# State-space stage: five of eight B products on GpSimd after the scans, three on VectorE from PSUM, and no pair additions

## The chip, the cores and the metric

The kernel is one launch on one core of a Trainium2 chip. The metric is the device time of a launch in microseconds; the kernel before took 2772.1 us in the median of 3 runs (2766.68 to 2773.61). The engines are called as the profile calls them: PE (TensorE, matrix products), PEld (its weight loads), DVE (VectorE), ACT (ScalarE), POOL (GpSimd), SP (SyncE, here the queue of transfers).

## The reference, cut to what matters

The whole is a decoder of two layers on x of 16 sequences x 112 steps x 256 features: a state-space layer, cross attention, a mixture of experts, an encoder, a second cross attention with a long convolution, and a coupled network. The change touches the first stage only:

```python
dt = softplus(x[:, :, 0:1] * W_dt + b_dt)
BC = einsum('bld,ed->ble', x, W_xp) + b_xp
Bm, Cm = BC[..., :16], BC[..., 16:]
# for every step t of a sequence
state = exp(A * dt_t) * state + dt_t * x_t * B_t     # 256 features x 16 states
y = einsum('bdn,bn->bd', state, C_t)
out = y @ W_out + b_out                              # then residual and layer norm
```

## The kernel before, in words

The stage is cut into eight units. A unit is one half c of the 256 features (128 partitions) and one quarter q of the 16 sequences (4 sequences x 112 steps = 448 columns): unit 0 is (c=0, q=0), unit 1 (c=1, q=0), unit 2 (c=0, q=1) and so on. "Even units" have c=0, "odd units" c=1. The 16 states of a unit lie side by side in `st_h` (two buffers, by the parity of the unit), and are handled as eight pairs of 896 columns.

For each unit:

- PE broadcasts the rows of B, one pair of states at a time, over 128 partitions into PSUM (L478, a matmul of a one-hot column with `bc_parts`). There is one such ring of two slots in PSUM, for B and for C (`RING`); a broadcast waits until the one two places before it has been used. ACT copies all eight B pairs to SBUF (`b_s`, L578), once per quarter, in the odd unit before. Only for unit 0 does DVE read the B pairs straight from the ring (L701).
- POOL multiplies the eight B pairs with u = dt * x (L774, u is kept in `XD`) and writes them into `st_h`. It does so for unit i+1 at the start of unit i.
- ACT computes the decays exp(A dt) into `dA` (L588, 16 instructions), which are needed by the next unit and wait for this unit's scans.
- DVE runs the recurrence as two scans of eight states (L682, 3584 columns), then multiplies eight pairs with C out of the ring (L718).
- POOL adds the two states of a pair for six of the eight pairs (L781, `ADDED` = 6).
- PE sums the states of the unit by matmuls with the identity into one bank of PSUM (L492): one matmul for each added pair and two for each of the other two, 10 in all. It does this at the start of the next unit, after that unit's first two B broadcasts, if it has any.

After the sum PE does the unit's window of other work (`shared_uses`): in even units the products z and bc for the next quarter (L412, L418), in units 4 and 6 also transposes (L462), and in all units the keys and values of two sequences for the next stage (L430, L440). In odd units the remaining B broadcasts stand between them. The last work of the unit is the C broadcasts; in odd units from 3 on, the projection W_out (L453) stands after the second of them (`late_uses`), and DVE adds the residual and takes the statistics (L732, L265, L268) before its C products.

In even units ACT turns z into a part of dt (L534, L535, L538) and copies bc (L549, L550); the logarithms of the softplus (L544) stand behind the window. DVE splits bc into bfloat16 parts between its two scans (L661 to L663, `split`) and computes dt and u after the C products (L670, L672, `step_sizes`, four instructions for the two units of the next quarter). The first two work on bc's 64 rows, the others on 128 x 448.

The order on each engine is written out by hand; the engines meet at semaphores. `ssm_claim` deals three banks of PSUM in turn to the products of the window, so one of them waits until the third before it has been copied.

Of the kernel before, what the change touches and what calls it, by code (L numbers as in the profile page):

```python
# [20 lines left out]
P = 128  # L21
# [13 lines left out]
def build(nc, dr, out):  # L35

    ctx = ExitStack()
    with ctx:
# [185 lines left out]
        pair_added = sem("pair_added")  # L224
# [66 lines left out]
        HALF, ADDED = 8, 6  # L291
# [38 lines left out]
        def copied_b(i):  # L330

            c, q = UNITS[i]
            if i == 0:
                return [(0, pair) for pair in range(8)]
            return [(q + 1, pair) for pair in range(8)] if c == KC - 1 and q + 1 < NQ else []
# [29 lines left out]
        for i in range(len(UNITS)):  # L365
            RING += [("b", x) for x in copied_b(i)] + [("c", (i, pair)) for pair in range(8)]
        RING_AT = {u: n for n, u in enumerate(RING)}
        SSM_USES = [("z", 0), ("z", 1), ("bc", 0)]
# [5 lines left out]
        def ring_wait(eng, kind, at):  # L374

            i, pair = at
            if kind == "direct":
                eng.wait_ge(bcast_used, pair + 1)
            elif kind == "c":
                eng.wait_ge(bcast_used, 8 + 8 * i + pair + 1)  # L380
            else:
                eng.wait_ge(b_copied, 8 * i + pair + 1)
# [25 lines left out]
        def ssm_pe(pe):  # L408
# [60 lines left out]
            def broadcast(kind, at):  # L469

                n = RING_AT[(kind, at)]
                if n >= 2:
                    ring_wait(pe, *RING[n - 2])
                i, pair = at
                q, first = (UNITS[i][1], 16) if kind == "c" else (i, 0)
                for m in range(2):
                    s = first + 2 * pair + m
                    last = pe.matmul(ps[2 * (n % 2) + m][:, 0:QT], ident16[0:96, s:s + 1].to_broadcast([96, P]),  # L478
                                     bc_parts[0:96, q % 2, :], start=True, stop=True)
                last.then_inc(bcast_ready, 1)  # L480

            def sum_states(i):

                for pair in range(8):
                    if pair < ADDED:
                        pe.wait_ge(pair_added, i * ADDED + pair + 1)
                    else:
                        pe.wait_ge(bcast_used, 8 + 8 * i + pair + 1)
                    if pair == 0 and i >= 1:
                        pe.wait_ge(y_copied, i)  # L490
                    for m in range(1 if pair < ADDED else 2):
                        last = pe.matmul(ps[4][:, 0:QT], ident[:, :], st_h[:, i % 2, 2 * pair + m, :],  # L492
                                         start=(pair == 0 and m == 0), stop=(pair == 7 and m == 1))
                    last.then_inc(y_ready, 1)
# [9 lines left out]
            for i, (c, q) in enumerate(UNITS):  # L504
# [15 lines left out]
                for pair in range(2, 8):  # L520
                    broadcast("c", (i, pair))
            for k in range(KC):
                turn(KC * (NQ - 2) + k)
# [4 lines left out]
        def ssm_act(act):  # L528
# [43 lines left out]
            def copy_b(at):  # L572
                q, pair = at
                n = RING_AT[("b", at)]
                act.wait_ge(bcast_ready, n + 1)
                if q >= 1:
                    act.wait_ge(b_mult, 16 * (q - 1) + pair + 1)
                act.copy(b_s[:, 2 * pair:2 * pair + 2, :], PS[:, 2 * (n % 2):2 * (n % 2) + 2, 0:QT])\  # L578
                    .then_inc(b_copied, 1)
# [18 lines left out]
            copies = {"z": magnitude, "bc": copy_both, "k": copy_keys, "v": copy_values, "xt": copy_turned}  # L598
# [12 lines left out]
            for i, (c, q) in enumerate(UNITS):  # L611
# [9 lines left out]
                if c == 0 and q + 1 < NQ:  # L621
                    logarithm(2 * q + 2)
                    logarithm(2 * q + 3)
# [31 lines left out]
        def ssm_dve(dve, link):  # L655
# [18 lines left out]
            def scan(i, half):  # L674
# [4 lines left out]
                else:  # L679
                    dve.wait_ge(b_mult, 8 * (i - 1) + 4 * (half + 1))  # L680
                h = st_h[:, i % 2, n, :].rearrange("p n k -> p (n k)")
                dve.tensor_tensor_scan(h, dA[:, n, :, :].rearrange("p n b t -> p (n b t)"), h, 0.0,  # L682
                                       ALU.mult, ALU.add).then_inc(scan_done, 1)

# [11 lines left out]
            u2 = u_f[:, 0:1, 0:QT].to_broadcast([P, 2, QT])  # L696
            dve.wait_ge(u_done, 1)
            for pair in range(8):
                n = RING_AT[("direct", (0, pair))]
                dve.wait_ge(bcast_ready, n + 1)  # L700
                dve.tensor_tensor(st_h[:, 0, 2 * pair:2 * pair + 2, :], PS[:, 2 * (n % 2):2 * (n % 2) + 2, 0:QT],  # L701
                                  u2, ALU.mult).then_inc(bcast_used, 1)
            step_sizes(1)
            for i, (c, q) in enumerate(UNITS):
# [3 lines left out]
                scan(i, 1)  # L708
                if late_uses(i):
# [37 lines left out]
        def ssm_pool(pool, link):  # L747
# [17 lines left out]
            for i in range(len(UNITS)):  # L765
                if i + 1 < len(UNITS):
# [3 lines left out]
                    for pair in range(8):  # L770
                        pool.wait_ge(b_copied, 8 * q + pair + 1)
# [23 lines left out]
        def xat_load(sp):  # L795
            sp.wait_ge(b_mult, 8 * (len(UNITS) - 1))
# [1856 lines left out]
```

## Time and profile before

| | |
|---|---|
| median of 3 runs | 2772.1 us (2766.68 to 2773.61) |
| profiled execution, its own time | 2774.99 us |
| its span | 2773.1 us |
| mean granted clock of PE | 0.823 |
| PE busy | 2245.8 us (81%) |
| DVE busy | 1609.1 us (58%) |
| POOL busy | 894.5 us (32%) |
| ACT busy | 736.0 us (27%) |
| state-space scans on DVE (L682) | 181.8 us in 16 instructions |
| B products on POOL (L774) | 166.4 us in 56 instructions |

Busy time is that in which an engine has an instruction under way, also while that instruction is held up at a port. The shares are means over stages that differ: the stage of the change ends some 360 us after the start of the span, and only its own waits say what bounds it. An instruction's time in brackets is the idle time of its engine before it, with what ended it.

### The profile page before, as it was taken

What the parts mean: (1) busy time and instruction counts of PE and PEld (TensorE: products, weight loads), DVE (VectorE), ACT (ScalarE), POOL (GpSimd) and SP (SyncE); (2) the same over time, 40 slices, a digit from 0 to 9 for tenths busy, and PEclk for the clock granted to TensorE, in tenths of its full rate; (3) what the DMA queues carried; (4) which work ended last, traced back from release to release, by engine and by line L of the source; (5) the groups of instructions that cost most, each with busy time, mean ns of one, the idle gap of its engine ahead of it and who ended that gap; (6) DMA issues with size and microseconds to landing.
All of it is one profiled execution on the core that took longest, in us unless ns stands there. A gap on an engine that the chain in (4) does not pass through costs nothing.

```text
span 2773.1 us, 36682 instructions
## 1 busy us (share of the span) xinstructions
PE 2245.8 (81%) x14852; PEld 1568.3 (57%) x14852; DVE 1609.1 (58%) x3034; ACT 736.0 (27%) x1387; POOL 894.5 (32%) x715
## 2 busy tenths in 40 slices
PE   7787778888787999799999999988657775866776
PEld 2343345566565666578888887776445453434432
DVE  7888834444442333355565655666399997555345
ACT  6545322222221121222222222222222221211122
POOL 7787349816110000534444343442200002111000
PEclk7888866656556999799999999999766767788987
DMA  4212213111111000100100100100150101400000
GB/s 133 80 50 79 80 43 106 34 51 34 40 32 46 1 1 1 73 1 1 60 2 1 60 1 1 45 1 1 54 103 26 34 26 28 94 0 0 1 0 27
DMA packets 63473, 100.52 MB, mean 36 GB/s; under 512 B 32301, under 2 KB 56870, under 8 KB 62150
## 3 DMA queue, kind: packets, MB, share of 16 engines
q1 hardware_dynamic: 63306, 98.18, 12.2%
q8 instruction: 119, 1.95, 0.3%
q14 instruction: 48, 0.39, 0.0%
HBM read 77.67 MB, written 20.50 MB: 35 GB/s over the span
## 4 chain that ended last, share of the span: by engine, by line
PE 62%; DVE 25%; DMA 4%; ACT 3%; issue 3%; POOL 3%; SPq 0%; POOLq 0%; DVEq 0%; ACTq 0%
PE PS L1421 7%; PE PS L1437 7%; PE PS L1177 4%; DVE st_h L682 4%; DVE top L2175 3%; PE PS L883 3%; PE PS L1156 3%; DVE w_s L2184 3%; PE PS L1338 3%; DMA enc_w<-v_all_scratch 3%; PE PS L896 2%; DVE XD L1038 2%; PE PS L2061 2%; DVE ln_st L265 2%; PE PS L933 2%
## 5 line engine op out<-in xcount | busy, mean ns | idle before, releaser
L284 POOL TENSOR_SCALAR ln_ve<-ln_mv 128x2 f32<-128x2 f32 (+1 forms) x91 | 20.2, 222 | 1523.4 <-DVE ln_mv L268 1523.4
L883 PE MATMUL PS<-enc_w,q_s 17*112 17x375 f32 x512 | 188.1, 795 | 78.0 <-DVE XD L1038 59.8
L1613 DVE TENSOR_TENSOR p_x<-PS,cols 128x1024 f32<-128x1024 f32 x112 | 129.3, 1218 | 147.7 <-PE PS L1383 147.6
L1038 DVE TENSOR_REDUCE XD<-PS 112x2 f32<-112x750 f32 x128 | 120.3, 940 | 161.0 <-PE PS L883 161.0
L1675 POOL TENSOR_TENSOR q_x<-q_f,cols 128x2048 f32<-128x2048 f32 x56 | 208.6, 3744 | 9.7 <-ACT q_f L1533 9.7
L682 DVE TENSOR_TENSOR_SCAN st_h<-dA,st_h 128x3584 f32<-128x3584 f32 x16 | 181.8, 11388 | 0.0
L896 PE MATMUL PS<-q_s,enc_w 17*125 17x112 f32 x1536 | 180.1, 388 | 1.1 <-ACT e_t L1006 1.1
L1006 ACT ACTIVATE e_t<-PS 125x672 f32<-125x672 f32 x128 | 93.6, 731 | 312.8 <-PE PS L896 312.8
L774 POOL TENSOR_TENSOR st_h<-b_s,XD 128x896 f32<-128x896 f32 x56 | 166.4, 3009 | 8.0 <-PE PS L492 6.8
L896 PEld LDWEIGHTS PS<-q_s,enc_w 17*125 17x125 f32 x1536 | 151.2, 279 | 2.1 <-issue 2.0
L1241 DVE SCALAR_TENSOR_TENSOR XA<-PS,gate_w,XA 112x256 f32<-112x256 f32 x128 | 61.9, 484 | 135.4 <-PE PS L1177 135.4
L1945 PE MATMUL PS<-dg,e_p 112*125 112x112 f32 x384 | 82.4, 409 | 71.3 <-ACT dg L2129 71.3
L883 PEld LDWEIGHTS PS<-enc_w,q_s 17*112 17x112 f32 x512 | 59.4, 250 | 131.9 <-DVE XD L1038 85.4
L478 PE MATMUL PS<-bc_parts,ident 96*128 96x448 bf16 x208 | 78.3, 478 | 62.2 <-DVE st_h L718 54.3
L1503 ACT ACTIVATE wb<-PS,cols 128x256 f32<-128x256 f32 x224 | 91.0, 473 | 141.1 <-PE PS L1421 141.1
L1945 PEld LDWEIGHTS PS<-dg,e_p 112*125 112x125 f32 x384 | 79.1, 320 | 82.9 <-issue 82.9
L1177 PE MATMUL PS<-wc,h_t 128*112 128x256 f32 x512 | 119.2, 388 | 2.4 <-DVE XA L1244 2.4
L1421 PE MATMUL PS<-wc 128*128 128x256 f32 x448 | 105.6, 396 | 10.4 <-ACT wc L1548 10.4
L1177 PEld LDWEIGHTS PS<-wc,h_t 128*112 128x112 f32 x512 | 92.4, 181 | 33.0 <-issue 14.3
L1421 PE MATMUL PS<-wc,enc_w 128*128 128x256 f32 x448 | 100.4, 382 | 9.5 <-ACT wc L1548 9.5
L1156 PE MATMUL PS<-XF,wc 128*128 128x448 f32 x256 | 103.6, 549 | 0.7 <-DVE gate_wt L1230 0.7
L1421 PEld LDWEIGHTS PS<-wc 128*128 128x128 f32 x448 | 87.6, 198 | 26.4 <-ACT wc L1548 14.0
(351 smaller groups left out, 4959.3 us busy)
## 6 DMA issues: line engine op xcount, KB each, us to landing
v_all_scratch<-v_st SPq DMA_DIRECT2D x16, 750.0 KB
enc_w<-v_all_scratch SPq DMA_DIRECT2D x16, 750.0 KB
t_ring<-k_scratch SPq DMA_DIRECT2D x8, 784.0 KB, 11.5
enc_w<-in_enc_w SPq DMA_DIRECT2D x2, 3072.0 KB, 10.4
wc<-in_enc_w SPq DMA_DIRECT2D x2, 3072.0 KB, 10.9
k_all_scratch<-k_st SPq DMA_DIRECT2D x16, 375.0 KB
enc_w<-k_all_scratch SPq DMA_DIRECT2D x64, 93.8 KB
ctx_k<-in_ctx SPq DMA_DIRECT2D x16, 281.2 KB
```

What stands on the lines that cost most here:

```text
L682: dve.tensor_tensor_scan(h, dA[:, n, :, :].rearrange("p n b t -> p (n b t)"), h, 0.0, ALU.mult, ALU.add).then_inc(scan_done, 1)
L774: pool.tensor_tensor(st_h[:, (i + 1) % 2, 2 * pair:2 * pair + 2, :], b_s[:, 2 * pair:2 * pair + 2, :], u2, ALU.mult).then_inc(b_mult, 1)
L883: ins = pe.matmul(ps[a][0:T, 0:S2], q_s[h, m, b * T:(b + 1) * T], k_s[h, b % 2, m, :], start=True, stop=True)
L896: ins = pe.matmul(ps[2 + a][0:JR, j * T:(j + 1) * T], k_s[h, b % 2, m, j * JR:(j + 1) * JR], q_s[h, m, b * T:(b + 1) * T], start=True, sto ...
L1038: dve.tensor_reduce(nm_w[0:T, g % 2, 64 * half + 16:64 * half + 49:32], PS[0:T, 0:2, 0:S2], AX.X, ALU.max, negate=True).then_inc(max_done, 1)
L1156: last = pe.matmul(ps[pair + m][:, 0:QT], w1_e[:, e, k, m * P:(m + 1) * P], XF[:, k, q * QT:(q + 1) * QT], start=(k == 0), stop=(k == KC - 1))
L1177: last = pe.matmul(bank, h_t[:, i % 2, k, b * T:(b + 1) * T], w2_e[:, e, k, :], start=(k == 0), stop=(k == KC - 1))
L1421: last = pe.matmul(ps[bank][:, (m % 2) * RT:(m % 2 + 1) * RT], w[:, k, m * P:(m + 1) * P], x1f[:, i % 2, k, :], start=(k == 0), stop=(k == ...
L1437: last = pe.matmul(ps[3][:, g * D:(g + 1) * D], h_ff[:, m, g * P:(g + 1) * P], w[:, m, :], start=(m == 0), stop=(m == 7))
L1613: last = dve.tensor_tensor(p_x[:, m, :, :, :], ps[1][:, m * P:(m + 1) * P].rearrange("p (h i) -> p h i", i=16).unsqueeze(2) .to_broadcast( ...
L1675: last = pool.tensor_tensor(q_x[:, c, :, :].rearrange("p t (h i) -> p t h i", i=16), q_f[:, k % 2, c, :].rearrange("p (t i) -> p t i", i=1 ...
L1945: last = pe.matmul(bank[0:JR, j * T:(j + 1) * T], e_p[:, XH * (b % 2) + h, j * JR:(j + 1) * JR], dg[:, b % 2, h, :], start=(h == 0), stop= ...
```

## The change

What it does:

- POOL takes five B pairs of each unit (`COPIED` = 5) and starts them only after both scans of the unit before are done (a wait on `scan_done`). DVE takes the other three from the ring in PSUM, right after its C products of the unit before (`multiply_b`). ACT copies five B pairs a quarter in place of eight.
- The pair additions on POOL and their semaphore are gone. PE sums 16 states by 16 matmuls.
- In even units the two logarithms are computed right after the second `magnitude`, ahead of the copy of bc, and `step_sizes` stands on DVE after the second scan, ahead of the C products.

```diff
@@ -288,7 +287,7 @@
-        HALF, ADDED = 8, 6
+        HALF, COPIED = 8, 5
...
         for i in range(len(UNITS)):
             RING += [("b", x) for x in copied_b(i)] + [("c", (i, pair)) for pair in range(8)]
+            if i + 1 < len(UNITS):
+                RING += [("direct", (i + 1, pair)) for pair in range(COPIED, 8)]
...
             def sum_states(i):
 
                 for pair in range(8):
-                    if pair < ADDED:
-                        pe.wait_ge(pair_added, i * ADDED + pair + 1)
-                    else:
-                        pe.wait_ge(bcast_used, 8 + 8 * i + pair + 1)
+                    pe.wait_ge(bcast_used, DVE_AT[("c", (i, pair))] + 1)
                     if pair == 0 and i >= 1:
                         pe.wait_ge(y_copied, i)
-                    for m in range(1 if pair < ADDED else 2):
+                    for m in range(2):
...
                 for pair in range(2, 8):
                     broadcast("c", (i, pair))
+                if i + 1 < len(UNITS):
+                    for pair in range(COPIED, 8):
+                        broadcast("direct", (i + 1, pair))
...
+            def magnitude_and_log(i):
+                magnitude(i)
+                if i % KC == KC - 1:
+                    logarithm(i - 1)
+                    logarithm(i)
+
-            copies = {"z": magnitude, "bc": copy_both, "k": copy_keys, "v": copy_values, "xt": copy_turned}
+            copies = {"z": magnitude_and_log, "bc": copy_both, "k": copy_keys, "v": copy_values, "xt": copy_turned}
...
-                if c == 0 and q + 1 < NQ:
-                    logarithm(2 * q + 2)
-                    logarithm(2 * q + 3)
                 if i + 1 < len(UNITS):
                     decay(i + 1, 0)
                     decay(i + 1, 1)
...
+            def multiply_b(i, pair):
+                c, q = UNITS[i]
+                at = RING_AT[("direct", (i, pair))]
+                if i >= 2:
+                    dve.wait_ge(y_ready, 8 * (i - 2) + pair + 1)
+                dve.wait_ge(bcast_ready, at + 1)
+                dve.tensor_tensor(st_h[:, i % 2, 2 * pair:2 * pair + 2, :], PS[:, 2 * (at % 2):2 * (at % 2) + 2, 0:QT],
+                                  u_f[:, c:c + 1, q * QT:(q + 1) * QT].to_broadcast([P, 2, QT]), ALU.mult)\
+                    .then_inc(bcast_used, 1)
...
                 scan(i, 1)
+                if c == 0 and q + 1 < NQ:
+                    step_sizes(2 * q + 2)
+                    step_sizes(2 * q + 3)
...
                     dve.tensor_tensor(h, PS[:, 2 * (n % 2):2 * (n % 2) + 2, 0:QT], h, ALU.mult)\
                         .then_inc(bcast_used, 1)
-                if c == 0 and q + 1 < NQ:
-                    step_sizes(2 * q + 2)
-                    step_sizes(2 * q + 3)
+                if i + 1 < len(UNITS):
+                    if i == 0:
+                        dve.wait_ge(u_done, 2)
+                    for pair in range(COPIED, 8):
+                        multiply_b(i + 1, pair)
...
                     pool.wait_ge(u_done, i + 2)
-                    for pair in range(8):
-                        pool.wait_ge(b_copied, 8 * q + pair + 1)
+                    pool.wait_ge(scan_done, 2 * (i + 1))
+                    for pair in range(COPIED):
+                        pool.wait_ge(b_copied, COPIED * q + pair + 1)
...
-                for pair in range(ADDED):
-                    h0, h1 = st_h[:, i % 2, 2 * pair, :], st_h[:, i % 2, 2 * pair + 1, :]
-                    pool.wait_ge(bcast_used, 8 + 8 * i + pair + 1)
-                    pool.tensor_tensor(h0, h0, h1, ALU.add).then_inc(pair_added, 1)
```

The order of DVE's instructions in unit 4 (even) up to the first scans of unit 5, before (L682 is the scan):

```order
L682 SCALAR_TENSOR_TENSOR st_h<-dA,st_h 128x3584
L661 TENSOR_TENSOR bc_f<-bc_f,bc_parts 64x448
L662 CAST bc_parts<-bc_f 64x448
L663 TENSOR_TENSOR bc_parts<-bc_f,bc_parts 32x448
L682 SCALAR_TENSOR_TENSOR st_h<-dA,st_h 128x3584
L718 TENSOR_TENSOR st_h<-PS,st_h 128x896 x8
L670 TENSOR_TENSOR dt_f<-dt_f,XD 128x448
L672 TENSOR_TENSOR XD<-dt_f,XF 128x448
L670 TENSOR_TENSOR dt_f<-dt_f,XD 128x448
L672 TENSOR_TENSOR XD<-dt_f,XF 128x448
L682 SCALAR_TENSOR_TENSOR st_h<-dA,st_h 128x3584 x2
```

and the same place of the changed kernel (L687 is the scan, L664 to L666 the split, L673 and L675 the step sizes, L732 the C products, L696 the B products from PSUM):

```order
L687 SCALAR_TENSOR_TENSOR st_h<-dA,st_h 128x3584
L664 TENSOR_TENSOR bc_f<-bc_f,bc_parts 64x448
L665 CAST bc_parts<-bc_f 64x448
L666 TENSOR_TENSOR bc_parts<-bc_f,bc_parts 32x448
L687 SCALAR_TENSOR_TENSOR st_h<-dA,st_h 128x3584
L673 TENSOR_TENSOR dt_f<-dt_f,XD 128x448
L675 TENSOR_TENSOR XD<-dt_f,XF 128x448
L673 TENSOR_TENSOR dt_f<-dt_f,XD 128x448
L675 TENSOR_TENSOR XD<-dt_f,XF 128x448
L732 TENSOR_TENSOR st_h<-PS,st_h 128x896 x8
L696 TENSOR_TENSOR st_h<-PS,XD 128x896 x3
L687 SCALAR_TENSOR_TENSOR st_h<-dA,st_h 128x3584 x2
```

The step sizes moved ahead of the C products, three B products came in behind those, and the split stands where it stood, between the scans.

ACT in the window of unit 4, before (L534 to L538 the second magnitude, L549 and L550 the copies of bc, L570 those of the transposes):

```order
L534 ACTIVATE XD<-PS,cols 128x448
L535 ACTIVATE dt_f<-PS,cols 128x448
L538 ACTIVATE XD<-XD 128x448
L549 ACTIVATE bc_parts<-PS,cols 96x448
L550 ACTIVATE bc_f<-PS,cols 64x448
L570 COPY XF<-PS 128x448 x2
```

and after (L544 are the logarithms):

```order
L534 ACTIVATE XD<-PS,cols 128x448
L535 ACTIVATE dt_f<-PS,cols 128x448
L538 ACTIVATE XD<-XD 128x448
L544 ACT_TABLE_LOAD
L544 ACTIVATE XD<-XD 128x448 x2
L549 ACTIVATE bc_parts<-PS,cols 96x448
L550 ACTIVATE bc_f<-PS,cols 64x448
L570 COPY XF<-PS 128x448 x2
```

A table load and the two logarithms now stand ahead of the copies of bc.

PE from the end of unit 4 to the first C broadcasts of unit 5, before (L478 are broadcasts, two to a pair; L492 the sum):

```order
L478 MATMUL PS<-bc_parts,ident 128x448 x20
L492 MATMUL PS<-st_h,ident 128x448 x10
L478 MATMUL PS<-bc_parts,ident 128x448 x2
L430 MATMUL PS<-ctx_t,wb 128x375 x2
L478 MATMUL PS<-bc_parts,ident 128x448 x2
L430 MATMUL PS<-ctx_t,wb 128x375 x2
L478 MATMUL PS<-bc_parts,ident 128x448 x2
L440 MATMUL PS<-wb,ctx_t 125x256 x4
L478 MATMUL PS<-bc_parts,ident 128x448 x2
L440 MATMUL PS<-wb,ctx_t 125x256 x2
```

and after (the sum is L489):

```order
L478 MATMUL PS<-bc_parts,ident 128x448 x26
L489 MATMUL PS<-st_h,ident 128x448 x16
L478 MATMUL PS<-bc_parts,ident 128x448 x2
L430 MATMUL PS<-ctx_t,wb 128x375 x2
L478 MATMUL PS<-bc_parts,ident 128x448 x2
L430 MATMUL PS<-ctx_t,wb 128x375 x2
L478 MATMUL PS<-bc_parts,ident 128x448 x2
L440 MATMUL PS<-wb,ctx_t 125x256 x6
```

The run of broadcasts ahead of the sum is longer by three pairs, the sum by six matmuls, and the window has three B broadcasts (pairs) in place of six.

## Rows read from the trace of the kernel before

**Rows 1.** Timeline of DVE, units 4 to 6: start, length, what, idle before.

```profile
188.37 26.11 DVE L682 TENSOR_TENSOR_SCAN st_h<-dA,st_h 128x3584 f32<-128x3584 f32 x1
214.40 0.59 DVE L661 TENSOR_TENSOR bc_f<-bc_f,bc_parts 64x448 f32<-64x448 f32 x1
...
215.98 7.61 DVE L682 TENSOR_TENSOR_SCAN st_h<-dA,st_h 128x3584 f32<-128x3584 f32 x1
223.52 8.47 DVE L718 TENSOR_TENSOR st_h<-PS,st_h 128x896 f32<-128x896 f32 x8
231.90 0.62 DVE L670 TENSOR_TENSOR dt_f<-dt_f,XD 128x448 f32<-128x448 f32 x1
...
234.29 16.98 DVE L682 TENSOR_TENSOR_SCAN st_h<-dA,st_h 128x3584 f32<-128x3584 f32 x2
258.48 0.76 DVE L732 TENSOR_TENSOR XA<-PS,XA 112x256 f32<-112x256 f32 x2 [7.21 <-PE PS L453]
...
262.66 8.47 DVE L718 TENSOR_TENSOR st_h<-PS,st_h 128x896 f32<-128x896 f32 x8
271.05 34.25 DVE L682 TENSOR_TENSOR_SCAN st_h<-dA,st_h 128x3584 f32<-128x3584 f32 x2
```

**Rows 2.** Timeline of POOL in unit 4.

```profile
190.65 16.34 POOL L774 TENSOR_TENSOR st_h<-b_s,XD 128x896 f32<-128x896 f32 x8
```

**Rows 3.** Timeline of DVE: the first scans of units 1, 2, 3 and 7.

```profile
67.69 16.95 DVE L682 TENSOR_TENSOR_SCAN st_h<-dA,st_h 128x3584 f32<-128x3584 f32 x2
...
106.22 24.98 DVE L682 TENSOR_TENSOR_SCAN st_h<-dA,st_h 128x3584 f32<-128x3584 f32 x1
...
151.01 16.98 DVE L682 TENSOR_TENSOR_SCAN st_h<-dA,st_h 128x3584 f32<-128x3584 f32 x2
...
313.60 15.13 DVE L682 TENSOR_TENSOR_SCAN st_h<-dA,st_h 128x3584 f32<-128x3584 f32 x2
```

**Rows 4.** Timeline of PE, units 4 and 5: sums, windows, C broadcasts.

```profile
187.12 9.94 PE L492 MATMUL PS<-st_h,ident 128*128 128x448 f32 x20
196.98 1.77 PE L412 MATMUL PS<-XF,rows 1*128 1x448 f32 x4
...
202.34 3.35 PE L430 MATMUL PS<-ctx_t,wb 128*128 128x375 f32 x8 [0.91 <-ACT bc_f L550]
...
214.22 0.92 PE L478 MATMUL PS<-bc_parts,ident 96*128 96x448 bf16 x4
...
232.76 9.30 PE L492 MATMUL PS<-st_h,ident 128*128 128x448 f32 x20
241.90 0.54 PE L478 MATMUL PS<-bc_parts,ident 96*128 96x448 bf16 x2
...
255.72 0.92 PE L478 MATMUL PS<-bc_parts,ident 96*128 96x448 bf16 x4
```

**Rows 5.** Windows of L492 alone: length, PE busy, PEld busy, granted clock, DMA.

```profile
237.00:241.90 4.90, 4.90 (x14) 2.28 (x12) 1.00 0.00 0
...
187.20:190.00 2.80, 2.80 (x4) 1.27 (x4) 0.50 0.00 0
```

**Rows 6.** Timeline of ACT in unit 4: magnitudes, copies of bc, logarithms.

```profile
198.04 0.63 ACT L534 ACTIVATE XD<-PS,cols 128x448 f32<-128x448 f32 x1 [0.41 <-PE PS L412]
...
201.05 0.63 ACT L549 ACTIVATE bc_parts<-PS,cols 96x448 bf16<-96x448 f32 x1
201.57 0.63 ACT L550 ACTIVATE bc_f<-PS,cols 64x448 f32<-64x448 f32 x1
...
214.81 1.28 ACT L544 ACT_TABLE_LOAD   x1
216.11 1.04 ACT L544 ACTIVATE XD<-XD 128x448 f32<-128x448 f32 x2
```

**Rows 7.** Timeline of DVE in unit 0: the split beside POOL's B products.

```profile
39.61 1.98 DVE L661 TENSOR_TENSOR bc_f<-bc_f,bc_parts 64x448 f32<-64x448 f32 x1 [2.42 <-ACT bc_f L550]
...
43.82 2.39 DVE L663 TENSOR_TENSOR bc_parts<-bc_f,bc_parts 32x448 bf16<-32x448 f32 x1
46.14 7.60 DVE L682 TENSOR_TENSOR_SCAN st_h<-dA,st_h 128x3584 f32<-128x3584 f32 x1
```

More of the change, by code:

```diff
@@ L223, in build @@
         ones_set = sem("ones_set")
-        pair_added = sem("pair_added")
         dA_ready, scan_done = sem("dA_ready"), sem("scan_done")
@@ L333, in copied_b @@
             if i == 0:
-                return [(0, pair) for pair in range(8)]
-            return [(q + 1, pair) for pair in range(8)] if c == KC - 1 and q + 1 < NQ else []
+                return [(0, pair) for pair in range(COPIED)]
+            return [(q + 1, pair) for pair in range(COPIED)] if c == KC - 1 and q + 1 < NQ else []
         def shared_uses(i):
@@ L366, in build @@
             RING += [("b", x) for x in copied_b(i)] + [("c", (i, pair)) for pair in range(8)]
+            if i + 1 < len(UNITS):
+                RING += [("direct", (i + 1, pair)) for pair in range(COPIED, 8)]
         RING_AT = {u: n for n, u in enumerate(RING)}
+        DVE_AT = {u: n for n, u in enumerate(u for u in RING if u[0] != "b")}
         SSM_USES = [("z", 0), ("z", 1), ("bc", 0)]
@@ L376, in ring_wait @@
             i, pair = at
[L377 to L380, printed above, removed]
+            if kind == "b":
+                eng.wait_ge(b_copied, COPIED * i + pair + 1)
             else:
-                eng.wait_ge(b_copied, 8 * i + pair + 1)
+                eng.wait_ge(bcast_used, DVE_AT[(kind, at)] + 1)
         def ssm_bank(kind, i):
@@ L474, in broadcast @@
                 i, pair = at
-                q, first = (UNITS[i][1], 16) if kind == "c" else (i, 0)
+                q, first = (i if kind == "b" else UNITS[i][1]), (16 if kind == "c" else 0)
                 for m in range(2):
@@ L576, in copy_b @@
                 if q >= 1:
-                    act.wait_ge(b_mult, 16 * (q - 1) + pair + 1)
+                    act.wait_ge(b_mult, COPIED * 2 * (q - 1) + pair + 1)
                 act.copy(b_s[:, 2 * pair:2 * pair + 2, :], PS[:, 2 * (n % 2):2 * (n % 2) + 2, 0:QT])\
@@ L679, in scan @@
                 else:
-                    dve.wait_ge(b_mult, 8 * (i - 1) + 4 * (half + 1))
+                    dve.wait_ge(b_mult, COPIED * (i - 1) + min(4 * (half + 1), COPIED))
+                    if half == 1:
+                        dve.wait_ge(bcast_used, DVE_AT[("direct", (i, 7))] + 1)
                 h = st_h[:, i % 2, n, :].rearrange("p n k -> p (n k)")
@@ L695, in ssm_dve @@
             step_sizes(0)
-            u2 = u_f[:, 0:1, 0:QT].to_broadcast([P, 2, QT])
             dve.wait_ge(u_done, 1)
             for pair in range(8):
[L699 to L702, printed above, removed]
+                multiply_b(0, pair)
             step_sizes(1)
@@ L795, in xat_load @@
         def xat_load(sp):
-            sp.wait_ge(b_mult, 8 * (len(UNITS) - 1))
+            sp.wait_ge(b_mult, COPIED * (len(UNITS) - 1))
             for i in range(2):
```

## The prediction

> **What bounds the kernel now.** I read the timeline of DVE first, then those of PE, ACT and POOL at the same places. Times inside a unit are counted from the start of its first scan, called t = 0; the span from one unit's first scan to the next is its period.
>
> The reader is to see in [rows 1] that even units and odd units have different limits. Unit 4 (even) is bound by DVE: its first scan takes 26.11 us where the second takes 7.61, because POOL's eight B products, back to back for 16.34 us [rows 2], stand in between; everything on DVE follows without a gap, and the period is 234.29 - 188.37 = 45.9 us. In unit 5 (odd) the two scans take 16.98 us (POOL is the one that is held up), and then DVE idles 7.21 us for the projection [rows 1]. PE bounds it: the sum starts at 232.76, a window without holes follows, and C products start at 262.66 [rows 4, 1]. Its period is 36.8 us. The other starts of scans [rows 3, 1] give periods of 38.5 (unit 1), 44.8 (unit 2), 37.4 (unit 3) and 42.6 (unit 6). So a gain at the port counts in units 2, 4 and 6 alone, and work added to PE counts in all odd ones.
>
> **The sizes.** One state matmul shows as two records. At the full clock 4.90 us hold about 13 whole records [rows 5], 0.38 each, 0.76 us a matmul; at half clock four records take 2.80 us or more, twice that. The sums before, 10 matmuls in 9.94 and 9.30 us [rows 4], start at half clock and end at full clock. The six matmuls that are added come behind, at full clock: 6 x 0.76 = 4.6 us a unit. A DVE product from PSUM takes 8.38 / 8 = 1.05 us (223.52 to 231.90), also while POOL is at work; three more are 3.15 us. A B broadcast in the window shows 0.54 us [rows 4], part of it over its neighbour's time; I take 0.4, so three fewer give back 1.2 us in units 1, 3 and 5.
>
> **Odd units.** The direct products are at the end of DVE's order, and PE's sum stands behind their broadcasts, so the sum of the unit just ended cannot start before they are nearly done. In unit 5 before, the sum began 0.86 us after the C products' end (231.90), while DVE spent 2.39 us on the step sizes before its scan: PE had that head start. With the step sizes moved, the scan follows the last product at once, and PE lacks it. Change of period: 2.4 (head start gone) + 4.6 (matmuls) - 1.2 (broadcasts) + 3.15 (products after the C products) = +8.9 us, for units 3 and 5. From 36.8 to 45.7: DVE's scans, free of POOL, end at 15.2 and buy nothing. POOL's five products run from 15.2 to 25.6 and are hidden. Unit 1 has no projection or statistics. Its sum starts at 0.9 and takes 9.1 + 4.6, the window is 255.72 - 241.90 - 1.2 = 12.6, the first C broadcast 0.5, and 11 products 11.55: 39.3 us, +0.8 on 38.5, since PE there also waited for POOL's additions before.
>
> **Even units.** The scans are free, but the split between them waits for bc, and bc comes behind the sum on PE and, now, behind the logarithms on ACT. Before, in unit 4, the sum started at -1.25 and z at 8.6; bc's last copy ended at 202.20, t = 13.8 [rows 4, 6], hidden by the long first scan. After: 13.8 + 4.6 (matmuls) + 2.3 (table load and two logarithms, 214.81 to 217.15 [rows 6], which now stand before the copies) = 20.7. DVE ends its first scan at 7.6 and then waits 13 us. This is the main step of this prediction: the stall at the port is replaced by a stall at bc. Then the split takes 1.6 (214.40 to 215.98; POOL now waits for the second scan, so it is not disturbed), and the second scan 7.5: 29.9. At that moment POOL starts five products, and the four step sizes (0.62 us each alone [rows 1]) run beside them. In unit 0 before, three small DVE instructions beside such products took from 39.61 to 46.14, 2.18 us each [rows 7]. I take the first as free, 0.65, and three at 2.2: 7.25. The C products start at 37.1. PE is ready: its keys wait for bc's copy as the 0.91 us before them show [rows 4], so the first C broadcast ends at 20.7 + (214.22 + 0.54 - 202.20 = 12.6) = 33.3. Eleven products, 11.55, end the unit at 48.7. The period of unit 4 grows by 2.8, that of unit 2, the same sum against 44.8, by 3.9.
>
> The step sizes have two ends: alone they take 2.5 us, and the C products then start at PE's 33.3 in unit 4 (-3.8 us) and at 32.4 in unit 2 (-4.7); if DVE is kept out until all five are through (as the scan of 26.11 was for 16.34), they take 0.65 + 5 x 2.04 + 3 x 0.62 = 12.7, +5.5 a place. I stay with [rows 7], the same two kinds of instruction side by side.
>
> The Trainium skill has this rule (SBUF — State Buffer, "SBUF: two separate sides"): a DVE instruction with two inputs in SBUF and a GpSimd instruction take turns at a shared port, whoever starts first holds it for the whole instruction. This case's rows agree for the scan; for the short ones, a full turn of POOL before each of four would give 4 x (2.04 + 0.62) = 10.7 us in place of 7.25, some 3.4 more in each of three units. The measured pitch of 2.18 decides.
>
> **The ends of the stage.** Unit 0: before, DVE waited 2.42 us for bc and split from 39.61 [rows 7]. The 2.3 us of logarithms are partly hidden there (ACT itself waited for PE; between 0 and 2.3, I take 1.1): 40.7, + 1.6 + 7.5 = 49.8, + 7.25 = 57.1, + 11.55 = 68.6 against 67.69: +0.9. Unit 6 has no z, no bc and no split. PE: -1.25 + 9.9 + 4.6 + the window of unit 4 without z, bc and the wait (214.22 - 196.98, less 3.3 for z's 1.77 and as much for bc, overlapping, less 0.9: 13.0) + 0.4 = 26.7, + 11.55 = 38.3 against 42.6: -4.3. Here alone the freed port pays. Unit 7 has no direct products: +4.6; the sum of unit 7 after it: +4.6.
>
> **The sum.** 0.9 + 0.8 + 3.9 + 8.9 + 2.8 + 8.9 - 4.3 + 4.6 + 4.6 = +31.1 us. On the profiled execution's 2774.99 (span 2773.1 and 1.9 around it) that is 2806; it lay 2.9 above the median, so for the median 2772.1 + 31.1 = 2803. Nothing behind the stage changes; its start is simply late. The decays are hidden: in even units ACT starts them when the window ends, near 33, plus a table load of 1.3 and 9 us of work, 44 < 48.7.
>
> **The rivals.**
> - *Step sizes undisturbed, clock sooner back* (same mechanism, low end). POOL starts late enough or gives way: -4.7, -3.8, and -4.7 in unit 0. That is +17.9. If the sums also ran at full clock from the start, which no sum before did, the most is the excess over 7.6 us, about 2 us in each of eight: +2.
> - *Step sizes locked out, or the clock held low by PE's longer idle* (high end). Three times +5.5 from above: +47.6. For the clock: in unit 4 PE now idles for bc some 3 us more in its window, and if half of a window of 12 us went at half clock, it would add 6, of which 4 are hidden by the step sizes.
> - *Faster: the port decides.* If the excess of the first scans came free, 17.4 us in unit 2 (24.98 - 7.61), 18.5 in unit 4 and 19.1 in unit 6 (34.25 less two free scans), that is 55 us; against it stand the 28.7 of the other terms and three products more in each of the three, 9.5. That would give -17, 2755. It decides only if bc is there before 7.6. Against it: the sum of 16 alone takes until 13.2 even by these rows, and PE's order puts z and bc behind it. It would need PE to sum in a third of the time. The mild form, bc ready at 18 and all else at its best, is the +2 above.
> - *Nothing to see.* Between +2 and +8, where every loss meets its low end.
>
> **How the numbers follow.** Forecast with its own range of 2795 to 2812: 0.62. Low rival (2780 to 2795): 0.18. High rival (above 2812): 0.11. Nothing to see, within 0.3% or 8.3 us, about what a measurement can tell: 0.06. Faster: 0.03. The range for 8 in 10 is 2787 to 2815. Slower 0.91, same 0.06, faster 0.03.
>
> **What would show it.** In the profile of the changed kernel: all 16 scans near 7.6 us; DVE idle before L664 for some 13 us in units 2 and 4, put down to ACT's bc_f; L489 as 32 records in 13 to 15 us; the step sizes at about 2.2 us each but the first; odd periods near 46, even 49, unit 6 near 38. Wrong would be: a split without a wait, step sizes of 0.6 us, or the sum of 16 at under 12 us.

## The result, and the profile after

The changed kernel takes 2809.86 us in the median of 4 runs (2805.92 to 2815.83), the kernel before beside it 2770.59. The ratio is 1.0123, with a 95% interval of 1.0097 to 1.0149, which is 34 us slower (27 to 41); the two medians lie 39 us apart. Forecast were 31 us and a median of 2803, with a range of 2795 to 2812: the measured one lies in the range, near its upper end. The profiled execution has a span of 2808.8 us (before 2773.1, a difference of 35.7).

The stage's end is the end of its last statistics (L268 before, L267 after, in DVE's timeline): 363.13 us before and 398.33 after, +35.2. What follows takes 2410.0 and 2410.5 us. So all but 0.5 us of the difference between the two profiled executions is in the state-space stage. Its periods in us, from the starts of first scans:

| unit | before | forecast | after |
|---|---|---|---|
| 0 | 38.1 | +0.9: 39.0 | 39.6 |
| 1 | 38.5 | 39.3 | 39.9 |
| 2 | 44.8 | 48.7 | 49.1 |
| 3 | 37.4 | +8.9: 46.3 | 46.3 |
| 4 | 45.9 | 48.7 | 50.8 |
| 5 | 36.8 | 45.7 | 45.5 |
| 6 | 42.6 | 38.3 | 37.1 |
| 7 to the stage's end | 49.5 | +9.2: 58.7 | 60.9 |

DVE's timeline of units 4 and 5 after (start, length, what, idle before), which answers to [rows 1]:

```profile
204.01 7.61 DVE L687 TENSOR_TENSOR_SCAN st_h<-dA,st_h 128x3584 f32<-128x3584 f32 x1
224.49 0.62 DVE L664 TENSOR_TENSOR bc_f<-bc_f,bc_parts 64x448 f32<-64x448 f32 x1 [12.87 <-ACT bc_f L550]
...
226.10 7.61 DVE L687 TENSOR_TENSOR_SCAN st_h<-dA,st_h 128x3584 f32<-128x3584 f32 x1
233.64 0.59 DVE L673 TENSOR_TENSOR dt_f<-dt_f,XD 128x448 f32<-128x448 f32 x1
234.26 2.39 DVE L675 TENSOR_TENSOR XD<-dt_f,XF 128x448 f32<-128x448 f32 x1
236.57 2.49 DVE L673 TENSOR_TENSOR dt_f<-dt_f,XD 128x448 f32<-128x448 f32 x1
239.10 2.39 DVE L675 TENSOR_TENSOR XD<-dt_f,XF 128x448 f32<-128x448 f32 x1
243.31 8.20 DVE L732 TENSOR_TENSOR st_h<-PS,st_h 128x896 f32<-128x896 f32 x8 [1.82 <-PE PS L478]
251.60 3.28 DVE L696 TENSOR_TENSOR st_h<-PS,XD 128x896 f32<-128x896 f32 x3
254.79 15.13 DVE L687 TENSOR_TENSOR_SCAN st_h<-dA,st_h 128x3584 f32<-128x3584 f32 x2
284.40 0.76 DVE L748 TENSOR_TENSOR XA<-PS,XA 112x256 f32<-112x256 f32 x2 [14.48 <-PE PS L453]
...
288.58 8.47 DVE L732 TENSOR_TENSOR st_h<-PS,st_h 128x896 f32<-128x896 f32 x8
297.15 3.28 DVE L696 TENSOR_TENSOR st_h<-PS,XD 128x896 f32<-128x896 f32 x3
300.34 15.13 DVE L687 TENSOR_TENSOR_SCAN st_h<-dA,st_h 128x3584 f32<-128x3584 f32 x2
```

The reader is to see the trade: the first scan fell from 26.11 us to 7.61, and 12.87 us of idle time stand behind it, ended by ACT's copy of bc. The step sizes take 2.4 us each but the first. In unit 5 the wait for the projection grew from 7.21 to 14.48 us.

PE's timeline of the same stretch, which answers to [rows 4]:

```profile
202.69 14.26 PE L489 MATMUL PS<-st_h,ident 128*128 128x448 f32 x32
216.88 1.77 PE L412 MATMUL PS<-XF,rows 1*128 1x448 f32 x4
...
224.60 6.23 PE L430 MATMUL PS<-ctx_t,wb 128*128 128x375 f32 x8 [3.28 <-ACT bc_f L550]
230.76 5.48 PE L440 MATMUL PS<-wb,ctx_t 128*125 128x256 f32 x12
...
242.66 0.92 PE L478 MATMUL PS<-bc_parts,ident 96*128 96x448 bf16 x4
...
255.65 13.38 PE L489 MATMUL PS<-st_h,ident 128*128 128x448 f32 x32
268.87 0.54 PE L478 MATMUL PS<-bc_parts,ident 96*128 96x448 bf16 x2
```

The sums take 14.26 and 13.38 us for 16 matmuls, where 10 took 9.94 and 9.30: 4.3 and 4.1 more. Behind the wait for bc PE's keys (L430) take 6.23 us where they took 3.35. A window on them has the reason (length; busy time of PE, PEld, DVE, ACT and POOL; granted clock; DMA share and GB/s):

```profile
224.60:230.80 6.20, 6.20 (x9) 2.01 (x9) 6.13 (x4) 1.27 (x3) 0.00 (x0) 0.50 0.00 0
```

The granted clock is 0.50, which is 1.2 GHz, after 3.28 us without a matmul. Ahead of that wait, from 209 to 221 us, it was 1.00.

ACT at the same place, which answers to [rows 6], has the logarithms ahead of bc:

```profile
221.08 1.28 ACT L544 ACT_TABLE_LOAD   x1
222.38 1.04 ACT L544 ACTIVATE XD<-XD 128x448 f32<-128x448 f32 x2
223.33 0.61 ACT L549 ACTIVATE bc_parts<-PS,cols 96x448 bf16<-96x448 f32 x1
223.84 0.61 ACT L550 ACTIVATE bc_f<-PS,cols 64x448 f32<-64x448 f32 x1
```

And POOL's products in units 4 and 5, which answer to [rows 2]: 11.62 us beside the step sizes, 10.23 alone.

```profile
233.84 11.62 POOL L791 TENSOR_TENSOR st_h<-b_s,XD 128x896 f32<-128x896 f32 x5 [39.48 <-DVE st_h L687]
...
270.05 10.23 POOL L791 TENSOR_TENSOR st_h<-b_s,XD 128x896 f32<-128x896 f32 x5 [24.59 <-DVE st_h L687]
```

### The profile page after: what moved, and what is told of

Same layout as the page of the kernel before. It is cut to its first block, busy times and chain, and to the rows that moved or that the text cites. A ratio compares the mean times of both kernels' runs of the same rounds, so it can differ in the third digit from the quotient of the medians.

```text
span 2808.8 us, 36848 instructions
## 1 busy us (share of the span) xinstructions
PE 2308.5 (82%) x14966; PEld 1594.4 (57%) x14966; DVE 1580.4 (56%) x3055; ACT 724.7 (26%) x1375; POOL 743.0 (26%) x646
## 3 DMA queue, kind: packets, MB, share of 16 engines
q8 instruction: 119, 1.95, 0.3%
## 4 chain that ended last, share of the span: by engine, by line
PE 65%; DVE 22%; ACT 4%; DMA 3%; issue 3%; POOL 2%; SPq 0%; POOLq 0%; DVEq 0%; ACTq 0%
PE PS L1434 7%; PE PS L1450 7%; PE PS L1190 4%; PE PS L489 4%; PE PS L896 3%; DVE top L2188 3%; PE PS L1169 3%; DVE w_s L2197 3%; PE PS L1351 3%; PE PS L909 2%; PE PS L2074 2%; DVE XD L1051 2%; DMA enc_w<-v_all_scratch 2%; PE PS L946 2%; DVE ln_st L264 2%
## 5 line engine op out<-in xcount | busy, mean ns | idle before, releaser
L896 PEld LDWEIGHTS PS<-enc_w,q_s 17*112 17x112 f32 x512 | 60.5, 255 | 130.4 <-DVE XD L1051 85.9
L478 PE MATMUL PS<-bc_parts,ident 96*128 96x448 bf16 x226 | 89.7, 500 | 47.7 <-DVE st_h L732 37.5
L791 POOL TENSOR_TENSOR st_h<-b_s,XD 128x896 f32<-128x896 f32 x35 | 75.9, 2201 | 200.3 <-DVE st_h L687 177.4
L687 DVE TENSOR_TENSOR_SCAN st_h<-dA,st_h 128x3584 f32<-128x3584 f32 x16 | 121.3, 7608 | 0.0
L489 PE MATMUL PS<-st_h,ident 128*128 128x448 f32 x256 | 112.2, 603 | 0.0
```

The lines of the kernel that those rows point to most:

```text
L896: ins = pe.matmul(ps[a][0:T, 0:S2], q_s[h, m, b * T:(b + 1) * T], k_s[h, b % 2, m, :], start=True, stop=True)
```

## The experiments

The span of one profiled execution also moves with what lies behind the stage: 2403 to 2417 us in the fourteen profiled kernels, which differ in the first stage alone. The stage's end is the sharper reading, and each part gives both; ratios are to the kernel before, with 95% intervals. The end comes from one trace of each kernel, so its own spread was not measured. Two things bound it: the first scan starts between 28.56 and 31.18 us, and units that an edit leaves alone repeat closely (units 5, 6 and 7 take 45.6, 37.1 and 60.9 us in the first experiment and 45.5, 37.1 and 60.9 in the changed kernel). Of the versions of the changed kernel, the first three have ratios whose intervals overlap with its own, 1.0097 to 1.0149; what these experiments show, they show in the units.

**The split behind both scans.**

```diff
                 scan(i, 0)
-                if c == 0 and q + 1 < NQ:
-                    split(q + 1)
                 scan(i, 1)
                 if c == 0 and q + 1 < NQ:
+                    split(q + 1)
                     step_sizes(2 * q + 2)
```

> The changed kernel, with the split moved behind both scans (ahead of the step sizes). Theory (in even units DVE stalls for bc between its scans, while the second scan could have run): the second scan runs at once, both end at 15.2 us; the split starts when bc comes, at 20.4; the C products of unit 2 start when PE is ready, near 31 instead of 37.4 (-6 us), unit 0 gains 3.5, unit 4 nothing, since PE's own window ends there at 39.3. Span 2799 (-9). Rival (the wait for bc costs nothing, PE bounds all even units): -0 to -2 us. Rival (the order of the two does not matter, bc is late for what follows in any case): unit 2 unchanged too.

Span 2803.1, stage end 389.69 (-8.6 on the changed kernel), ratio 1.0094 (1.0068 to 1.0121). Unit 2 fell from 49.1 to 40.8 us and unit 4 stayed (50.8 and 51.1). The theory has the direction of both, and 6 us for the 8.3 of unit 2: there the split now took 6.5 us beside POOL, and the step sizes behind it ran alone in 2.5. Unit 0 did not gain its 3.5: there the split and the step sizes both ran beside POOL. The stall at bc between the scans costs in unit 2; in unit 4 PE's slowed window covers it, and DVE waits 10.68 us for the first C broadcast.

**z and bc ahead of the sum.**

```diff
+                order = window_order(i)
+                while i >= 1 and order and order[0][0] in ("z", "bc"):
+                    kind, at = order.pop(0)
+                    shared[kind](at)
                 if i >= 1:
                     sum_states(i - 1)
-                for kind, at in window_order(i):
+                for kind, at in order:
```

(and the same with `copies` and `copy_y` on ACT)

> The changed kernel, with z and bc (PE) and their magnitudes, logarithms and copies (ACT) ahead of the sum of states and the copy of y in units 2, 4 and 6. Theory (bc comes late because it stands behind the sum of 16): bc is there at about 7 us, DVE does not wait between its scans, PE does not idle before the keys and keeps its full clock, and the C products start when PE is ready, near 30. Periods of units 2 and 4 fall from 49.1 and 50.8 to about 41.5: span 2790 (-17 to -19). Rival (the sum's length itself, not its place, is what counts on PE): only the part of DVE's wait that PE's window does not cover, -8.

Span 2798.3, stage end 385.09 (-13.2), ratio 1.0076 (1.0048 to 1.0104). The span is 8 us above the 2790 expected, though units 2 and 4 take 41.8 and 42.9 us, near the 41.5 expected, and DVE no longer idles between its scans. The keys of unit 4 are at full speed again:

```profile
215.94 3.29 PE L430 MATMUL PS<-ctx_t,wb 128*128 128x375 f32 x8
```

The other units gave some of it back (unit 5 takes 46.3 for 45.5, unit 6 37.5 for 37.1), which I did not follow further.

**No wait for the scans on POOL.**

```diff
                     pool.wait_ge(u_done, i + 2)
-                    pool.wait_ge(scan_done, 2 * (i + 1))
```

> The changed kernel without POOL's wait on scan_done: its five products may run into the scans as before the change. Theory (the freed port buys nothing where DVE waits for bc or for PE anyway, and the wait makes the step sizes collide with POOL): scans become longer again by up to 10.4 us in some units, the step sizes fall from 2.4 to 0.6 us each, unit 2 gains about 5 us, the others about 0: span 2803 (-5). Rival (undisturbed scans are worth their time): even periods grow by 5 to 10 us each, span 2825 or more.

Span 2803.6, stage end 390.22 (-8.1), ratio 1.01 (1.0076 to 1.0123). The first scans of units 2 and 4 stay at 7.6 us without the wait (two scans take 16.96 for 15.13 in units 1, 3, 5 and 6). That is more than the theory had said: not even the length of these first scans needed it. Unit 2 gained 5.9 us, with step sizes of 0.6 us each. Within the changed kernel the wait is a loss, by the stage's end; the ratio is too near that of the changed kernel to say it.

**The pair additions back on POOL.**

```diff
-        HALF, COPIED = 8, 5
+        HALF, COPIED, ADDED = 8, 5, 6
...
-                    for m in range(2):
+                    for m in range(1 if pair < ADDED else 2):
...
+                for pair in range(ADDED):
+                    h0, h1 = st_h[:, i % 2, 2 * pair, :], st_h[:, i % 2, 2 * pair + 1, :]
+                    pool.wait_ge(bcast_used, DVE_AT[("c", (i, pair))] + 1)
+                    pool.tensor_tensor(h0, h0, h1, ALU.add).then_inc(pair_added, 1)
```

> The changed kernel with the pair additions back on POOL for six pairs, and 10 matmuls in PE's sum. Theory (six matmuls of 0.76 us stand in the chain of every unit, in odd ones directly, in even ones through bc; POOL can add beside DVE's products from PSUM): every period falls by about 4.6 us, the end too: 8 x 4.6, span 2772 (-37), as before the change. Rival (POOL's additions come late behind its five products and run into the next scans or hold PE's sum up, as in units 0 and 1 of the kernel before): the gain is under 20 us.

Span 2769.2, stage end 359.21 (-39.1), ratio 0.9985 (0.9967 to 1.0002). Units 1 to 6 fell by 4.7, 5.7, 4.7, 5.7, 4.6 and 4.0 us, and unit 7 with the end by 11.4. Unit 0 did not gain (39.8 for 39.6), and its first scan started 1.3 us later. The six extra matmuls of each sum are worth as much as the whole loss, in this kernel. What is left of the change then is hard to tell from the kernel before (the stage ends 3.9 us sooner, the ratio's interval holds 1): units 3 and 5 take 41.6 and 40.9 us for 37.4 and 36.8, units 2 and 6 43.4 and 33.1 for 44.8 and 42.6.

**The kernel before with one part alone: PE sums all 16 states.**

```diff
-        HALF, ADDED = 8, 6
+        HALF, ADDED = 8, 0
...
-                for pair in range(ADDED):
+                for pair in range(0):
```

> The kernel before, with one part of the change alone: PE sums all 16 states and POOL adds no pairs. Theory (the six matmuls stand in the chain of PE-bound units; even units have no use for the time): units 3, 5 and 7 and the end each grow by 4.6 us; even units change only as POOL's products meet the scans otherwise, -2 to -3 each: span 2785 (+12). Rival (the additions on POOL were as costly as the matmuls, by the port): no change or a gain, 2760 to 2773.

The theory missed: 2785 was expected, the span is 2763.4, the stage ends at 356.50 (-6.6 on the kernel before), ratio 0.9989 (0.9973 to 1.0005). The odd units do lose as expected: unit 3 takes 41.0 us for 37.4, unit 5 41.2 for 36.8, unit 7 with the end 60.5 for 49.5. But units 2, 4 and 6 take 40.9, 40.7 and 33.6 us for 44.8, 45.9 and 42.6, and units 0 and 1 gain 3.4 each. The medians do not tell this version from the kernel before. DVE's and POOL's timelines of its unit 2:

```profile
98.78 7.62 DVE L682 TENSOR_TENSOR_SCAN st_h<-dA,st_h 128x3584 f32<-128x3584 f32 x1
116.14 0.76 DVE L661 TENSOR_TENSOR bc_f<-bc_f,bc_parts 64x448 f32<-64x448 f32 x1 [9.74 <-ACT bc_f L550]
```
```profile
100.61 30.31 POOL L774 TENSOR_TENSOR st_h<-b_s,XD 128x896 f32<-128x896 f32 x8 [5.83 <-PE PS L492]
```

The eight products still have no wait for the scans, and they start 1.83 us after the scan, where they started 1.13 us after it in unit 2 of the kernel before (107.35 and 106.22); yet the first scan takes 7.62 us. So it was not the place of the products alone that kept it from the port in the kernel before: POOL was already at work when the scan came, with the additions of the odd unit, and went on into the products without a gap. POOL's timeline of the kernel before, just ahead of the row of [rows 2], shows it (DVE's scan came at 188.37):

```profile
184.11 6.58 POOL L781 TENSOR_TENSOR st_h<-st_h 128x448 f32<-128x448 f32 x6
```

**The logarithms and step sizes back in their old places.**

```diff
             def magnitude_and_log(i):
                 magnitude(i)
-                if i % KC == KC - 1:
-                    logarithm(i - 1)
-                    logarithm(i)
...
+                if c == 0 and q + 1 < NQ:
+                    logarithm(2 * q + 2)
+                    logarithm(2 * q + 3)
                 if i + 1 < len(UNITS):
                     decay(i + 1, 0)
```

(and on DVE `step_sizes` stands behind the three B products again)

> The changed kernel with the logarithms again behind the window on ACT and the step sizes again behind DVE's products. Theory (the logarithms delay bc by 2.3 us in front of a DVE that waits for it, the step sizes stand beside POOL's products at 2.4 us each, and moved ahead they take PE's head start of 2.4 us from every odd unit): unit 0 -3.3, unit 2 -5, unit 4 -6.7, units 1, 3, 5 -2.4 each: span 2787 (-22). Rival (the place of the step sizes is indifferent, only the 2.3 us before bc count): -7.

Span 2788.3, stage end 374.77 (-23.6), ratio 1.0053 (1.0031 to 1.0075), as the theory said. Units 0, 2 and 4 fell by 3.5, 6.9 and 6.3 us, units 1, 3 and 5 by 2.8, 3.0 and 1.8. The early step sizes cost on both sides: 7.8 us of DVE beside POOL in front of the C products, and the head start of PE in the next unit. The edit moves the logarithms and the step sizes together, so the even units' gain is not split between them; the odd units' gain and the size of the whole rule out the rival of -7.

This run and the fourth experiment together say what slows PE's keys in unit 4. With all 16 matmuls and the logarithms behind the window, the wait ahead of the keys is short and they run fast; with 10 matmuls and the logarithms ahead of bc, the wait is as in the changed kernel and so is the time of the keys. Here are first the keys of this run, then those of the fourth experiment:

```profile
205.93 3.35 PE L430 MATMUL PS<-ctx_t,wb 128*128 128x375 f32 x8 [0.92 <-ACT bc_f L550]
```
```profile
205.56 6.23 PE L431 MATMUL PS<-ctx_t,wb 128*128 128x375 f32 x8 [3.29 <-ACT bc_f L554]
```

So the slow window comes with the logarithms' place, not with the longer sum.

**All eight B products on POOL.**

```diff
-        HALF, COPIED = 8, 5
+        HALF, COPIED = 8, 8
...
-                    if half == 1:
+                    if half == 1 and COPIED < 8:
```

> The changed kernel with all eight B products on POOL, after the scans (COPIED = 8), none on DVE from PSUM. Theory (three products of 1.05 us stand at the end of DVE's chain, while POOL is idle in odd units): -3.15 + 1.2 for the copies and broadcasts in odd units, in even ones POOL's eight end 17.6 us after the scans and hold the next scan by 1 to 2 us: -16, span 2793. Rival (POOL's longer run collides with the scans and starves them, as in the kernel before): even units +5 or more, span 2810 or above.

Span 2786.7, stage end 376.94 (-21.4), ratio 1.004 (1.002 to 1.006). Each unit from 0 to 6 gained 2.2 to 4.3 us, mostly the three products at the end of DVE's chain. POOL's eight took 17.8 us in even units and touched only the next first scan there, by 1.7 us at most (16.82 for 15.13 for two, in unit 1). That is more than the 16 expected, since the even units gained more than the odd ones (3.1 to 4.3 us for 2.2 to 2.8), which was not followed further.

**A version drawn from the theory: additions, bc first, six products on POOL.**

> A version drawn from the theory: pair additions back on POOL, z and bc ahead of the sum, six B products on POOL after the scans and two on DVE. Theory: even periods near 36 us (before 45 and 46), odd ones near 41 (before 37), unit 7 and the end as before the change: span 2749, under both kernels. Rival (POOL with six products and six additions is late and holds back the next scans or the sum in even units): even periods of 43 or more, span 2765 or above.

It has the edits of the second and fourth experiment with `COPIED` = 6. Span 2762.0, stage end 345.63 (-17.5 on the kernel before), ratio 0.999 (0.997 to 1.001): its 2749 was missed by 13. About half of that is the rest of the program, 2416.4 us in that execution for 2410.0, and half lies in the stage. The runs show no difference from the kernel before that can be measured. The additions of unit 2 ran into the scans of unit 3, six in 13.91 us, and PE's sum waited for them (unit 3: 43.4 us; unit 5, without such a meeting, 40.8).

**Additions where they are over before the next scan.**

The kernel before, with `ADDED` as a list by unit, read as `ADDED[i]`:

```diff
-        HALF, ADDED = 8, 6
+        HALF, ADDED = 8, [0, 0, 6, 0, 6, 0, 6, 6]
```

> The kernel before, with POOL's pair additions kept only for units 2, 4, 6 and 7 and PE summing 16 states for units 0, 1, 3 and 5. Theory (the additions of an odd unit run straight into POOL's products and keep the next even unit's first scan from the port for 16 us; those of an even unit are over before the next scan and spare the PE-bound odd unit 4.6 us): the even first scans take 7.6 us, even periods are near 41, odd ones 37 to 38, the end is as before: span 2745 (4 x 4.6 under the 2763 of the version without any additions, 28 under the kernel before). Rival (the additions take as much by the port as the matmuls, wherever they stand): 2760 or more. Rival (the lock-out comes from the products' own place, not from additions ahead of them): even first scans of 24 us again.

Span 2760.0 for the 2745 expected, ratio 0.9944 (0.9921 to 0.9967). It bears out the reading of the kernel before with a sum of 16. Its first scan of unit 4, behind an odd unit without additions:

```profile
176.84 7.62 DVE L682 TENSOR_TENSOR_SCAN st_h<-dA,st_h 128x3584 f32<-128x3584 f32 x1
```

With additions back in units 2 and 4 it stays short, and units 3 and 5 are at 36.3 and 36.0 us. The stage's end, 356.88, is worse than expected by one unit: the additions of unit 6 met the scans of unit 7.

```profile
286.87 21.22 POOL L781 TENSOR_TENSOR st_h<-st_h 128x448 f32<-128x448 f32 x6
```

Six additions took 21.22 us where they take 6.6, and PE's sum waited. Read one by one, DVE and POOL took turns here. The scan came at 289.54, in the third addition, and got in when that was over; the fourth addition waited for the first scan and the fifth for the second:

```profile
290.16 8.45 POOL L781 TENSOR_TENSOR st_h<-st_h 128x448 f32<-128x448 f32 x1
```
```profile
298.57 8.44 POOL L781 TENSOR_TENSOR st_h<-st_h 128x448 f32<-128x448 f32 x1
```

**Without those of unit 6.** `ADDED` = [0, 0, 6, 0, 6, 0, 0, 6].

> As the last version with additions in some units, but only in units 2, 4 and 7. In that one the additions of unit 6 began just as the scans of unit 7 did, took 21 us and held PE's sum and so DVE's C products of unit 7 (43 us after its first scan, where 31 is seen without additions). Theory: unit 7's C products start near 31 again, the rest as there: the stage ends 12 us sooner, near 343 (before: 361), span 2748. Rival (unit 7 waits for something else): unchanged at 2760.

(This expectation and that of the last experiment count the end of the stage 2.6 us earlier than the text does.) The stage ends at 346.87, 10.0 us sooner (12 expected); unit 7 and the end take 55.1 us for 67.3, and the first scan of the stage started 1.35 us later. The span is 2760.3, as the rest took 2413.4 here and 2403.1 there; the ratio is 0.9936 (0.9912 to 0.996). It beats both kernels, by little: 2760.63 us in the median, beside 2774.17 for the kernel before.

**The wait for the scans alone, on top of the sum of 16.** The version with 16 matmuls and no additions, plus `pool.wait_ge(scan_done, 2 * (i + 1))`.

> The kernel before, with PE summing all 16 states, no additions, and POOL's eight products waiting for both scans of the unit. Theory (without additions the scans are already free, so the wait buys nothing; it puts the products beside the step sizes and the next scan): even periods +4 us each against the version without the wait, odd ones unchanged: span 2775 (+12 on 2763). Rival (the wait frees the split and the scans in even units): the same as without it or below, 2755 to 2763.

Span 2767.1, but the stage ends at 350.50, 6.0 us before that without the wait; ratio 0.9961 (0.9943 to 0.9978). Even periods grew by 3.5 and 3.9 us as expected, but unit 3 fell by 6.8 and unit 5 by 4.6, for the step sizes, now 2.4 us each, hold DVE between its last C product and its scan, while PE already sums. A pair of units takes 78.6 us for 81.9. By the traces, the theory that the wait buys nothing falls here; the intervals of the two versions, 0.9973 to 1.0005 without the wait and 0.9943 to 0.9978 with it, just overlap. What the units show is this: the split runs undisturbed (1.6 us for 5.3), which shortens the way to the C products. In units 2 and 4 of the changed kernel that gain could not come: in the version of it without the wait POOL was through at 126.04 us in unit 2, and bc came at 128.26.

**The same with additions in unit 7 alone.**

> The kernel before with the sum of 16 and POOL's wait for both scans, and additions for unit 7 alone. Theory (in unit 7 no scans follow, so POOL's additions are free and spare the end 4.6 us; the wait frees the split and lets PE run ahead during the longer step sizes): the stage ends 4 to 5 us sooner than with the wait and no additions (353.9 in the version without the wait, 347.9 with it), near 343: span 2762 against 2767. Rival (nothing to gain at the end): 2767.

Unit 7 and the end take 56.0 us for 60.5, the 4.5 expected. The stage ends at 349.28 all the same, as unit 3 and unit 4 took 2.4 us more between them, and the ratio is 0.9943 (0.9927 to 0.9959), 2758.26 us.

## Why the prediction was right

- **Even units: the stall at the port becomes a stall at bc.** Right. Forecast 13 us of waiting, shown 12.80 (unit 2) and 12.87 (unit 4). Two experiments take it away from between the scans, by the order on DVE and by the order on PE; they gain 8.3 and 7.3 us in unit 2, where 6 and 7.6 were worked out.
- **Six matmuls, 4.6 us.** Right in size for units 1 to 6 (4.0 to 5.7 when they were taken out again). Unit 7 and the end gave +11.4 for 9.2. The last sum takes 13.97 us for 7.90, 6.1 more and not 4.6: it starts here at a granted clock of 0.63 (378 to 382 us), where it was 0.95 before (348.3 to 352). What made the clock later was not tried.
- **Odd units: +8.9.** Right: +8.9 and +8.7. Its terms were moved one by one: the matmuls gave 4.7 and 4.6, the head start 3.0 and 1.8 (with the logarithms moved too), the products less broadcasts 2.7 and 2.7, where 4.6, 2.4 and 1.95 stood in the sum. They add up to 10.4 in unit 3 and 9.1 in unit 5, so they are not quite independent.
- **Step sizes, 2.2 us beside POOL.** Shown: 2.39 to 2.51. Four of them took 7.8 us for the 7.25 in the sum. By the rule of the Trainium skill (SBUF — State Buffer, "SBUF: two separate sides") the prediction had 10.7; the pitch read from the trace was nearer. The turns of that rule are there all the same: POOL's second to fifth product started 2.3 to 2.4 us apart (236.12, 238.54, 240.97), one step size to each, where they take 2.04 alone. The 10.7 was too long because it had a turn ahead of the first step size, which waited for nothing, and 0.62 us on top of each. The prediction also says that the rows agree with the rule for the scan. They do not wholly: by the rule a scan that comes while POOL is at work waits for one instruction, and the scan of 26.11 us waited for a run of them.
- **Unit 4.** Forecast +2.8, shown +4.9. The step that is short is the clock: I had put the half-speed window at 6 us, 4 of them hidden, in the high rival and not in the sum. The keys and values ran 6.2 us longer, and 1.82 us of it came through as DVE's wait for the first C broadcast. What started it was the 3.28 us wait for bc behind the logarithms: with these moved back the wait was 0.92 and the keys took 3.35 us.
- **Why the even units were slow before.** The prediction said that POOL's eight products stood in the way, so that moving the products is what frees the scans. That is not what the runs show: the products start about as soon after the scan as they did, and the scan is free once the additions ahead of them are gone. Of all that the change does, dropping the additions of the odd units was enough for that; dropping all additions, alone, takes 6.6 us off the stage.
- **The size as a whole.** +35.2 in the stage for +31.1: unit 4 gave 2.1 us more than forecast and unit 7 with the end 2.2, unit 6 gave 1.2 less, the others differ by 0.6 or less. Part of the agreement is that these misses have both signs.

## What to carry to other kernels

Before an instruction is moved to free one wait, ask what the waiting instruction's neighbour waits for: a scan that becomes 18.5 us shorter is worth nothing where its successor's input comes 13 us later, behind a sum that the same change made longer. Where two engines share a port, look at who is at work when the other arrives, and move the work that runs into that moment: here 6.6 us of additions ahead of 16.3 us of products were what kept the other engine out. When a short step is moved across an engine's order, count the head start that it gave to the engine behind.

## What the runs showed of the hardware that was not expected

In units 2, 4 and 6 of the kernel before, a scan that came while POOL was in a run of instructions was kept out until the whole run was over: 26.11 us for 7.6 in unit 4, in a run of 6.58 us of additions and 16.34 us of products. One that came when POOL was idle (98.78 us, POOL's start 100.61, in the version with a sum of 16) took 7.62, and it was POOL's first product that waited, 7.66 us for 2.04.

This does not hold for every run of instructions. Three short DVE instructions passed one by one between products, at 2.2 us each, and the scan behind them, at 46.14 us in [rows 7], took 7.60 with POOL's products still under way. The first scan of unit 1 in the same trace came at 67.69, in the fifth of six additions with eight products behind them; it got in after that one, and the sixth addition waited for it:

```profile
68.71 8.44 POOL L781 TENSOR_TENSOR st_h<-st_h 128x448 f32<-128x448 f32 x1
```

The scans of unit 7 with additions in unit 6 (289.54 us) got in the same way. So both outcomes occur in runs of the same two kinds of instruction, and what decides between them was not tried. What the experiments show is that the lock-out goes when the additions ahead of the scan are dropped.

The part of the program behind the stage took 2403 to 2417 us, though nothing in it differed. A gain of 10 us ahead of it can be out of sight in a single execution: when the additions of unit 6 were dropped, the stage's end moved by 10.0 us and the span by 0.3.
